# Four of nine point slices per dense chunk are added on VectorE, and TensorE turns five slices where it turned nine

## The reference, cut to what matters

```python
samp = gather(y0, x0) * (wy0 * wx0)[..., None] + gather(y0, x0 + 1) * (wy0 * wx1)[..., None] \
     + gather(y0 + 1, x0) * (wy1 * wx0)[..., None] + gather(y0 + 1, x0 + 1) * (wy1 * wx1)[..., None]
out = jnp.einsum('bhwgkc,bhwgk->bhwgc', samp, weights)      # a sum over the 9 points k
```

## Time and profile before

| | us |
|---|---|
| median of 3 runs | 2552.23 (2549.48 to 2552.93) |
| profiled execution, its own time | 2552.92 |
| its span | 2551.1 |
| PE busy | 2269.3 (89%) |
| DVE busy | 1895.3 (74%) |
| POOL busy | 1668.8 (65%) |
| ACT busy | 1223.9 (48%) |

### The profile page before, as it was taken

One profiled execution on the slowest core, in us unless ns is written; L12 is line 12 of the kernel. 1 busy time (PEld: TensorE's weight loads), 2 busy tenths in 40 slices (PEclk: granted clock), 3 DMA queues, 4 the chain that ended last, 5 costly groups with the idle time before them and its releaser, 6 DMA issues.

```text
span 2551.1 us, 61174 instructions
## 1 busy us (share of the span) xinstructions
PE 2269.3 (89%) x18976; PEld 2157.1 (85%) x18976; DVE 1895.3 (74%) x4404; ACT 1223.9 (48%) x3974; POOL 1668.8 (65%) x1797
## 2 busy tenths in 40 slices
PE   1487799999999999999999999999999999999887
PEld 1387698988988898898889898889999998999877
DVE  5576687777877777787777777877778878877543
ACT  1133354554554545455455455545554555455455
POOL 3777777777777776766666776767777777775000
PEclk6798899999999999999999999999999999999999
DMA  8522222222222222222122222212112111111000
GB/s 192 159 58 59 65 67 60 59 65 67 65 66 61 63 58 63 66 61 61 56 56 58 67 62 60 64 54 58 57 58 59 57 58 57 57 57 43 9 23 5
DMA packets 219754, 158.70 MB, mean 62 GB/s; under 512 B 149530, under 2 KB 186988, under 8 KB 219596
## 3 DMA queue, kind: packets, MB, share of 16 engines
q0 software_dynamic: 55296, 113.36, 14.9%
q1 hardware_dynamic: 164300, 43.73, 7.6%
HBM read 138.90 MB, written 18.04 MB: 62 GB/s over the span
## 4 chain that ended last, share of the span: by engine, by line
PE 56%; DVE 14%; issue 12%; ACT 8%; POOL 7%; DVEq 1%; SPq 1%; DMA 0%; ACTq 0%; POOLq 0%
PE Y L1598 14%; PE DGB L1496 12%; PE Z L1587 11%; POOL got L897 7%; PE DGB L1539 4%; DVE acc L1207 3%; ACT hid L1410 3%; ACT L1395 3%; PE N L1641 2%; PE N L1659 2%; PE N L1506 2%; DVE made L1059 2%; PE N L1546 2%; DVE turns L1277 1%; PE N L1667 1%
## 5 line engine op out<-in xcount | busy, mean ns | idle before, releaser
L897 POOL DMA_INDIRECT got<-patches,ranks x1728 | 1653.8, 957 | 639.3 <-issue 495.5
L1410 ACT ACTIVATE hid<-Z,b 128x128 f32<-128x128 f32 x2048 | 577.0, 372 | 501.0 <-PE Z L1587 499.5
L1059 DVE TENSOR_TENSOR made<-TW,tent 128x1152 f32<-128x1152 f32 x512 | 690.9, 1351 | 17.9 <-PE DGB L1496 14.4
L1496 PE MATMUL DGB<-ident,made 128*128 128x128 f32 x4608 | 596.4, 275 | 56.5 <-DVE bias L1125 41.2
L1598 PE MATMUL Y<-w,hid 128*128 128x128 f32 x4096 | 576.9, 284 | 68.4 <-DVE acc L1207 60.3
L1598 PEld LDWEIGHTS Y<-w,hid 128*128 128x128 f32 x4096 | 505.4, 194 | 109.9 <-DVE acc L1207 60.7
L1496 PEld LDWEIGHTS DGB<-ident,made 128*128 128x128 f32 x4608 | 523.1, 142 | 70.4 <-DVE bias L1125 42.0
L1587 PE MATMUL Z<-xt_m,w 128*128 128x128 f32 x4096 | 539.2, 278 | 0.5 <-ACT xt_m L1392 0.5
L1587 PEld LDWEIGHTS Z<-xt_m,w 128*128 128x128 f32 x4096 | 498.0, 194 | 6.9 <-issue 6.6
L1345 ACT ACTIVATE spread<-DGB 128x256 f32<-128x256 f32 x256 | 97.9, 382 | 389.4 <-PE DGB L1496 383.6
L1136 DVE TENSOR_TENSOR got<-got,TW 128x1152 f32<-128x1152 f32 x192 | 258.6, 1347 | 23.3 <-DMA got<-patches,ranks 22.1
(11 more groups left out here) (192 smaller groups left out, 2329.0 us busy)
## 6 DMA issues: line engine op xcount, KB each, us to landing
got<-patches,ranks POOLq DMA_INDIRECT x1728
vwin<-vpad SPq DMA_DIRECT2D x320, 40.0 KB
patches<-arena SPq DMA_DIRECT2D x92, 96.0 KB
w<-in_L_ffn_w SPq DMA_DIRECT2D x2, 2048.0 KB
patches<-got SPq DMA_DIRECT2D x38, 96.0 KB, 2.2
vpad<-vt SPq DMA_DIRECT2D x128, 16.0 KB
out<-X SPq DMA_DIRECT2D x32, 64.0 KB
X<-in_x SPq DMA_DIRECT2D x1, 576.0 KB, 4.4
```

The source lines that it names most:

```text
L897: pool.indirect_dma_start(out=got[:, q, j * PATCH:(j + 1) * PATCH], out_offset=None, in_=table, in_offset=bass.IndirectOffsetOnAxis(ap=ran ...
L1059: v.tensor_tensor(made[:, n % MADE, :].rearrange("p (k y x) -> p k y x", k=K, y=CHUNK), weighed.rearrange("p (k y) -> p k y", k=K)[:, :, c ...
L1410: ins = a.activation(hid[:, e % 2, c, :], Z[e % 2][:, c * P:(c + 1) * P], ACT.Relu, bias=b1[n][:, e * FC + c:e * FC + c + 1])
L1496: ins = pe.matmul(DGB[:, n % 2 * P:(n % 2 + 1) * P], made[:, n % MADE, k * P:(k + 1) * P], ident[:, :], is_transpose=True, start=(k == 0), ...
```

## The change

VectorE gets a second instruction per chunk. It adds slices 4 to 7 of `made` onto slices 0 to 3, in place, 512 elements per partition, and has a step p(n) of its own, which waits for m(n). TensorE waits for p(n) where it waited for m(n), and turns the slices 0, 1, 2, 3 and 8.

```diff
-        dense_v = Steps(sem("dense_v"), " ".join(f"m{n}" for n in range(2 * CHUNKS)))
+        dense_v = Steps(sem("dense_v"), " ".join(f"m{n} p{n}" for n in range(2 * CHUNKS)))
...
                                     tent[g][:, 0, :, :].unsqueeze(2).to_broadcast([P, K, CHUNK, W]), ALU.mult)\
                         .then_inc(*dense_v.step(f"m{n}"))
+                    v.wait_ge(*dense_v.done(f"m{n}", t))
+                    v.tensor_tensor(made[:, n % MADE, 0:4 * P], made[:, n % MADE, 0:4 * P],
+                                    made[:, n % MADE, 4 * P:8 * P], ALU.add).then_inc(*dense_v.step(f"p{n}"))
...
                 if part == "sum":
-                    pe.wait_ge(*dense_v.done(f"m{n}", t))
+                    pe.wait_ge(*dense_v.done(f"p{n}", t))
...
-                    for k in range(K):
+                    for k in (0, 1, 2, 3, K - 1):
                         ins = pe.matmul(DGB[:, n % 2 * P:(n % 2 + 1) * P], made[:, n % MADE, k * P:(k + 1) * P],
                                         ident[:, :], is_transpose=True, start=(k == 0), stop=(k == K - 1))
```

## The result

| | us |
|---|---|
| before, median of 4 runs beside it | 2551.4 (2549.48 to 2552.93) |
| after, median of 4 runs | 2754.84 (2753.27 to 2757.54) |
| after : before | 1.0799, 95% interval 1.0780 to 1.0818 |
| forecast | 2626, range 2560 to 2676 |

The change costs 203 us where 74 were forecast. The direction is right. The size is not: the time lies 79 us above the range, and 59 above the dearest rival.

The account below looks back on a forecast made before the run. PE was taken to bound the kernel before, DVE after; 2552.9 us + 48 (first loop) + 13 (second loop) + 12.5 (slots 0 to 3, 30 and 31) = 2626, 80% range 2560 to 2676.

Parts of the forecast that it names:

- the dearest rival: TensorE's granted clock falls in the loops as PE idles more: 2696 us in all, chance 0.12.
- Additions and transposes: Per chunk, a 689 ns addition puts 0.72 us on DVE (11.5 per slot); four fewer transposes take 0.44 off PE.
- The waits of the earlier trace for PE and ACT go to nearly nothing: DVE's 7.7 us per slot of waits for PE and ACT shrink to 0.3, as additions stand ahead of them.
- 0.3 us ahead: At L1306, the tightest wait, its producer on PE (L1659) was to end 0.3 us ahead of it.
- The step-by-step account: One slot followed in order: PE gets p(n) at once, ends the sum 0.54 us later, finishes other products before DVE needs them.
- The stall: At the first loop's branch, 3.0 us of DVE's 4.5 us issue stall stay per pass; none in the second loop.
- two blocks of 256: Cited instruction-memory sizes, by which both loops would be too long after the change; kept among the rivals.
- The small gaps: Short gaps between dependent DVE instructions and a few small waits: 4.0 us per slot, not filled by more work.
- The clock: Rival: granted clock dips, some where DVE waits for PE (L1306), 2.2 us per slot more, 2696 us; chance 0.12.
- The start and the gathers: Slots 0 to 2: additions mostly hidden in 22 us of gather waits, +6; slot 3 +1; gathers cost nothing in loops.
- the 980 of the signs: Sign that additions slow GpSimd: gathers with a mean over 980 ns.
- 77.4: First-loop slot, us: 74.1 of DVE work and gaps, 3.0 stall, 0.3 remaining waits, for 74.85 before; second loop 74.1.

Follow-up runs that it names:

- eight fillers: The changed kernel with eight empty semaphore increments ahead of VectorE's first loop: 2726.16 us, ratio 1.0688.
- the extra products: The second changed kernel with the eight Z products of expert 5 in the first pass made three times over: 2668.24 us, ratio 1.0462.
- the second changed kernel: The changed kernel with the starting increments of two semaphores moved from VectorE's list to SyncE's: 2674.93 us, ratio 1.0488.
- the first of the kernels with four additions: The changed kernel with addition and five slices only for chunks 5, 7, 12, 13 of a slot, nine slices for the others: 2509.99 us, ratio 0.9828.
- 2508: The kernel before with eight empty semaphore increments ahead of VectorE's loops: 2507.92 us, ratio 0.9829.
- the early a3: Accumulations a0 to a3 early in both passes, against the kernel with additions for chunks 5, 7, 12, 13 and late copy (2492.10 us): 2508.94 us.
- the late-copy kernel: The second changed kernel with, on DVE alone, the copy L1309 behind the product and addition of chunk 14: 2608.22 us, ratio 1.0211.

## Why the prediction fell short

1. **Additions and transposes: right.** 695 ns for the forecast 689; a slot's DVE work 69.8 for 70.1. The saved transposes were forecast to bring nothing to a DVE-bound slot; the kernel that turns all nine slices after the addition is not slower but 15 us faster.
2. **The failed step: "The waits of the earlier trace rows for PE and ACT go to nearly nothing", L1306 with its producer "0.3 us ahead".** For L1179 and L1166 it holds. L1306 (now L1309), for which 0.3 us per slot was kept, waits 4.1 us in the mean of the first loop and 3.3 in the second. The step-by-step account took PE to need from DVE only the `made` of each chunk. PE's product for expert 4 also needs a3. In the kernel before, PE and then DVE:

```profile
1208.06 0.65 PE L1483 MATMUL CV<-wo,arena 128*128 128x288 f32 x2
1208.58 1.16 PE L1598 MATMUL Y<-w,hid 128*128 128x128 f32 x8
...
1207.41 1.12 DVE L1207 SCALAR_TENSOR_TENSOR acc<-Y,route,acc 128x128 f32<-128x128 f32 x3
...
1215.21 0.69 DVE L1306 COPY turns<-N 128x512 f32<-128x512 f32 x1 [3.48 <-PE N L1659]
```

   a3 ends at 1208.53 and the product starts at 1208.58. The distance is 0.05 or 0.06 us in all 19 slots, the same as in the changed kernel, where PE stands still 2.3 us for a3. So a3 had no slack before, yet no list of idle times shows it: PE was busy just until then. (PE's waits for acc of up to 1.9 us in these slots lie at other places, the longest behind the stall at the branch.) The copy's wait is then the way from a3 to the copy through PE, less what DVE has to do meanwhile: 6.7 - 3.2 = 3.5 before, and 6.2 - 3.6 = 2.6 after at full clock. Additions ahead of a3 move both ends and take nothing from it; only the one behind it, and the transposes saved on the way, shorten it. The fallen clock puts 1.5 back in the mean: 4.1. Shown by moving a3 ahead of one pair (-72 us), and by four additions at two places (71 us between them).
3. **The stall: right in kind, 1.05 us per pass too small.** One remained, the second went, the second loop had none. 4.05 in place of 3.0; the list ends two instructions into the fourth packet, not one. Two instructions fewer take it away (-80 us), eight fillers bring it to the forecast's 3.0. One argument beside it was wrong. The second body of 284, which goes round without a fetch, was held against the two blocks of 256 that the prediction had cited; 284 is less than 512, so it says nothing, and by such blocks neither loop need have been too long after the change. What does speak against them is in the last section.
4. **The small gaps: 4.0 forecast, 5.3 found** (13.6 - 4.2 - 4.05) in the two slots. 0.5 of it was forecast with the pairs: L1065's 17.6 us of idle time over 32 slots are 0.55 per slot. The others of 0.2 to 0.7 us (waits for ACT's sd_m, for L982, before L1042) stay.
5. **The clock: a rival at 2.2 us per slot.** It fell where DVE waits for PE, at the copy, as the rival said: from PE's product for expert 4 to the copy it is 7.6 us in the first loop and 6.9 in the second, in the mean, and 6.2 where the clock did not fall. That is 1.5 and 0.7 per slot, 32 us in all, within the waits of point 2. What it cost in the whole time is open: the extra products took it away at this place in the second changed kernel, and gave 7 us.
6. **The start and the gathers: right.** The first L1280 comes at 295.85 for 288.25, 7.6 later where 6 + part of slot 3 were forecast, and DVE's waits for gathers in 100:300 fell from 22.1 to 2.2. The gathers' mean is 987 ns, over the 980 of the signs, and in the loops DVE waits for none of them.

The sum. In the two slots 83.4 for 77.4 is 6.0 = 3.9 (the copy's wait, with its clock) + 1.05 (stall) + 1.3 (gaps) - 0.3 (busy). Over all, 19 x (83.0 - 77.4) + 7 x (77.3 - 74.1) + 1.6 (the start) = 130 for the 129 that were missed; 93 of them are the copy's wait (19 x 3.8 + 7 x 3.0) and 20 the stall. The range failed for the same reason: in no rival did PE wait for a3, and even the clock's 2696, which the range left out, is 59 us short.

What stays open: why the first of the kernels with four additions is not under 2508, beyond that the waits move; why the early a3 harms there; what the clock costs in all; and the 8 us of the fillers' 29.

## What to carry to other kernels

Before work is put on an engine, list what the *other* engines need from it in that stretch, from the waits in the program, and take for each the time from the end of the result to the start of its user. A list of idle times is not enough: here the user started 0.05 us after the result in every slot and had no idle time to show. A user without slack is moved by the new work ahead of its result, and a wait of the loaded engine behind that user is not filled by work put ahead of the result. Where two engines are near balance, the place of an addition matters as much as its length (71 us here for the same four). And look at the instruction queue: a loop that fetches its list in every pass may be cured by a shift of a few instructions, which alone gave 1.7% here, and any edit to such a kernel moves that boundary too.

## What the runs showed of the hardware

- The time of a loop depends on where its list lies. Eight semaphore increments ahead of it took the packets from 119 to 29 and 43 us off the kernel before; two instructions fewer took 80 us off the changed one. A body of 326 instructions went round without a fetch at one place (30 packets), and fetched two further on (121). The Trainium skill, "Runtime: NRT & Kernel Launch", section "Instruction fetch mechanics", has refills of 256 instructions and two such blocks held; what it says of a taken branch whose target is outside agrees with the 3.0 to 4.05 us here. Its sizes do not fit both shifts. By them the body of 293 of the kernel before fetches, and eight further on does not, only if the branch's target is one of the last eight instructions of a block. The change moves the target by 65, and a body of 326 would fit two blocks from there; it fetched. Packets of 128 with three held fit every run here: by the count of instructions, those whose first body ends within three packets of the one with its target have 29 to 31 packets in all, the others 119 to 121. The size of a packet is worked out from these shifts and the 8 KB, not seen by itself.
- A stall behind the branch has more than one length: 4.05 us with two instructions beyond the third packet, 3.0 with ten, and 2.99 + 1.56 in two parts in the kernel before.
- TensorE's granted clock: eight products behind an idle time of 2.33 us last 2.08 us where they take 1.06 to 1.16 else; the granted clock there is 0.50, the lower of its two levels (1.2 and 2.4 GHz). Behind the same idle time (2.33 us) in the late-copy kernel they last 1.16, so the idle time before it does not decide alone. The kernel with more work for PE had a granted clock of 1.00 and 0.98 in two slots where the changed one had 0.90 and 0.94, and was 15 us faster.
